# Graph layer plus experts on one core: the tiles of a three-block product pass are dealt out 11, 13, 10 instead of 10, 14, 10, and in the third block TensorE sums five tiles per product instead of four

## The reference, cut to what matters

```python
def _L1_gnn_ref(x_nodes, x_edges, path_coeffs, src, dst, path_indices):
    x1 = x_nodes[src].reshape(-1, N_SEG, EXTENT)
    x2 = x_edges.reshape(-1, N_SEG, EXTENT)
    i1, i2, i3 = (path_indices[:, 0], path_indices[:, 1], path_indices[:, 2])
    contrib = path_coeffs[None, :, None] * x1[:, i1, :] * x2[:, i2, :]
    edge_out = zeros.at[:, i3, :].add(contrib)          # 64 paths into 16 segments
    out = zeros.at[dst].add(edge_out.reshape(-1, 512))  # edges into nodes
    return out
```

## Time and profile before

| | |
|---|---|
| median of 3 runs | 276.3 us (276.22 to 276.34) |
| the profiled execution, its own time | 276.32 us |
| its span, first to last instruction | 274.5 us |
| PE busy | 263.9 us (96%) |
| DVE busy | 223.8 us (82%) |
| ACT busy | 168.5 us (61%) |
| first block, first multiply to that of the second | 89.99 to 125.48 us |
| second block | 125.48 to 181.25 us |
| third block, up to the final scatters | 181.25 to 225.77 us |
| final scatters | 225.77 to 238.95 us |

### The profile page before, as it was taken

How to read it: one execution, slowest core, us unless ns; L and a number is a source line. 1 busy time by engine, 2 the same in 40 slices (tenths; PEclk the granted TensorE clock), 3 DMA queues, 4 the chain that set the end, 5 groups by cost and what they waited for, 6 DMA issues and landing times.

```text
span 274.5 us, 5669 instructions
## 1 busy us (share of the span) xinstructions
PE 263.9 (96%) x1639; PEld 185.3 (67%) x1639; DVE 223.8 (82%) x662; ACT 168.5 (61%) x341; POOL 39.6 (14%) x52
## 2 busy tenths in 40 slices
PE   6999999999999899998999999989999989999996
PEld 4566798886444799996778786756665654468633
DVE  5977665299657999999999999999999987655272
ACT  6931341010526999978878787499999719343260
POOL 4000150060006766661000000000000000000000
PEclk9999999999999999999999999999999999999999
DMA  6699990000014755555342000014444439000002
GB/s 205 213 412 405 445 420 25 0 2 1 1 38 127 204 171 153 156 157 152 92 142 76 2 1 1 2 36 141 162 152 152 148 87 352 21 2 2 2 0 76
DMA packets 12592, 33.91 MB, mean 124 GB/s; under 512 B 3345, under 2 KB 3602, under 8 KB 12306
## 3 DMA queue, kind: packets, MB, share of 16 engines
q1 hardware_dynamic: 10482, 26.73, 27.1%
q0 software_dynamic: 2080, 6.82, 8.9%
HBM read 32.50 MB, written 1.05 MB: 122 GB/s over the span
## 4 chain that ended last, share of the span: by engine, by line
PE 83%; DVE 9%; issue 3%; ACT 2%; DVEq 1%; DMA 1%; ACTq 0%; SPq 0%
PE psum L1348 15%; PE psum L1295 14%; PE psum L1249 10%; PE psum L1351 8%; PE psum L1273 5%; DVE big L1040 4%; PE psum L1278 4%; PE psum L1301 3%; PE psum L1422 3%; PE psum L1448 3%; PE psum L1192 3%; PE psum L1178 2%; PE psum L1132 2%; PE psum L1339 2%; PE psum L1230 1%
## 5 line engine op out<-in xcount | busy, mean ns | idle before, releaser
L1295 PE MATMUL psum<-big,dst_oh 128*128 128x512 f32 x108 | 50.7, 594 | 0.5 <-DVE big L1040 0.5
L606 ACT ACTIVATE prod<-edges,coef_b 128x320 f32 (+1 forms) x78 | 43.8, 594 | 10.6 <-PE psum L1351 9.1
L1348 PE MATMUL psum<-prod,ident 128*128 128x128 f32 x160 | 32.1, 295 | 1.0 <-DVE prod L1030 0.9
L1348 PEld LDWEIGHTS psum<-prod,ident 128*128 128x128 f32 x160 | 24.5, 190 | 10.2 <-issue 9.4
L1030 DVE TENSOR_TENSOR prod<-big,prod 128x320 f32<-128x320 f32 (+1 forms) x53 | 29.4, 556 | 0.5 <-issue 0.3
L1295 PEld LDWEIGHTS psum<-big,dst_oh 128*128 128x128 f32 x108 | 18.7, 191 | 15.1 <-issue 14.3
L1249 PE MATMUL psum<-edges,big 128*128 128x256 f32 x128 | 28.3, 381 | 0.0
L1040 DVE TENSOR_TENSOR big<-big,prod 128x64 f32 (+2 forms) x80 | 26.8, 335 | 0.0
L606 ACT ACTIVATE xparts<-edges,coef_b 128x320 f32 (+1 forms) x48 | 26.1, 589 | 1.0 <-PE psum L1348 0.8
L1249 PEld LDWEIGHTS psum<-edges,big 128*128 128x128 f32 x128 | 24.1, 190 | 3.5 <-issue 0.3
L471 POOL DMA_INDIRECT big<-xn_rows,big x16 | 17.0, 1061 | 30.5 <-DMA xn_rows<-xn 23.5
(11 more groups left out here) (223 smaller groups left out, 529.4 us busy)
## 6 DMA issues: line engine op xcount, KB each, us to landing
big<-in_w SPq DMA_DIRECT2D x3, 2048.0 KB, 16.6
edges<-in_edge SPq DMA_DIRECT2D x1, 3584.0 KB, 23.9
edges<-in_f SPq DMA_DIRECT2D x7, 512.0 KB, 3.4
edges<-in_edge SPq DMA_DIRECT2D x1, 2560.0 KB, 23.7
edges<-in_edge SPq DMA_DIRECT2D x5, 512.0 KB, 3.5
edges<-in_f SPq DMA_DIRECT2D x1, 2560.0 KB, 9.8
big<-in_f SPq DMA_DIRECT2D x4, 512.0 KB, 3.6
big<-in_gnn_w SPq DMA_DIRECT2D x1, 1024.0 KB, 6.1
```

Of the source, the lines that this page charges most:

```text
L606: nc.scalar.activation(slot(n)[:, 0:BLOCKS[b], :], segment(edges_of(b), single_column(words, p)), ACT.Copy, scale=coef_b[:, p:p + 1]).then ...
L1295: last = mm(bank[2 + h], dst_oh[:, n % DR, h * P:(h + 1) * P], tile_sums(b, t), start=False, stop=False)
L1348: last = mm(path_sums(to), ident[:], product[:, 0:PT].rearrange("p t u -> p (t u)"), start=False, stop=True, skip_group_check=True)
```

## The change

The first block has 11 tiles, the second 13, the third 10. `KEPT` is [8, 6, 5]: in the third block one product of 160 columns takes five tiles, and DVE adds five tiles instead of six. The 16 segments' sums of five tiles lie three to a bank, in banks 4, 5, 6, 7, 0, 1 (`last_sums`), so PE clears six banks there and ACT makes six copies of them at the end. Because banks 0 and 1 are used again, ACT copies all six banks of the second block at one place, after the scale of path 7 (`LEAD = 8`). ACT clears five rows (`BLOCKS[2] - KEPT[2]`) instead of six. One tile of the last layer's weights `f2` moves to another room.

```diff
-    BLOCKS = [10, 14, 10]
-    FIRST = [0, 10, 24]
-    KEPT = [8, 6, 4]
+    BLOCKS = [11, 13, 10]
+    FIRST = [0, 11, 24]
+    KEPT = [8, 6, 5]
...
+    PER_BANK = 512 // (KEPT[2] * U)
...
-    LEAD, REST_LEAD = 6, 11
+    LEAD = 8
...
+        def last_sums(k):
+            b = psum[:].bitcast(mybir.dt.uint8).rearrange("p (s e) -> p s e", e=4 * U)
+            at = nc.s_assert_within((k * 171 + 2048) // 32 % 128, 0, 128 - KEPT[2], ...)
+            return b[:, bass.ds(at, KEPT[2]), :].rearrange("p o e -> p (o e)").bitcast(F32)
...
-            return [4, 5, 6, 7] + list(range(PT2[b]))
+            return [4, 5, 6, 7] + list(range(PT2[b] if b < NB - 1 else 2))
...
+                    if b == NB - 1:
+                        n = min(PER_BANK, NS - PER_BANK * i)
+                        nc.scalar.activation(
+                            kept_sums[b][:, :, PER_BANK * U * i:U * (PER_BANK * i + n)]...,
+                            bank[q][:, 0:n * KEPT[b] * U]..., ACT.Copy)\
+                            .then_inc(block_out, 1)
...
                 if b == 2 and p == LEAD - 1:
-                    copy_sums(1, 0, PT)
-                if b == 2 and p == REST_LEAD - 1:
-                    copy_sums(1, PT, 8)
+                    copy_sums(1, 0, PT + PT2[1])
...
-                    last = mm(path_sums(to), ident[:], product[:, 0:PT].rearrange("p t u -> p (t u)"),
-                              start=False, stop=True, skip_group_check=True)
-                    if KEPT[b] > PT:
+                    if b == NB - 1:
+                        last = mm(last_sums(to), ident[:], product[:, 0:KEPT[b]].rearrange("p t u -> p (t u)"),
+                                  start=False, stop=True, skip_group_check=True)
+                    else:
+                        mm(path_sums(to), ident[:], product[:, 0:PT].rearrange("p t u -> p (t u)"),
+                           start=False, stop=True, skip_group_check=True)
                         last = mm(more_sums(b, to), ident[:], product[:, PT:KEPT[b]].rearrange("p t u -> p (t u)"),
                                   start=False, stop=True, skip_group_check=True)
```

More of the change, by code:

```diff
@@ L43, in graph_and_experts @@
     PE_TILES = 8
-    PT2 = [k - PT for k in KEPT]
+    PT2 = [k - PT for k in KEPT[:2]]
+    PER_BANK = 512 // (KEPT[2] * U)
     ROW_PATHS = -(-NP // 3)
@@ L86, in more_sums @@
             return product_sums(psum[:, 0:NS * PT2[b] * U], PT2[b] * U, k)
+        def last_sums(k):
+            b = psum[:].bitcast(mybir.dt.uint8).rearrange("p (s e) -> p s e", e=4 * U)
+            at = nc.s_assert_within((k * 171 + 2048) // 32 % 128, 0, 128 - KEPT[2],
+                                    skip_runtime_bounds_check_because="three segments to a bank, six banks around the scatters")
+            return b[:, bass.ds(at, KEPT[2]), :].rearrange("p o e -> p (o e)").bitcast(F32)
         def carve(base, dt_size=4):
@@ L177, in graph_and_experts @@
         kept_sums = [sum_room[0][:, 0:KEPT[0], :], x1g[1][:, 0:KEPT[1], :], sum_room[0][:, 0:KEPT[2], :]]
-        rest_sums = [sum_room[0][:, KEPT[0]:, :], sum_room[1], sum_room[0][:, KEPT[2]:, :]]
+        rest_sums = [sum_room[0][:, KEPT[0]:, :], sum_room[1], sum_room[0][:, KEPT[2]:BLOCKS[2], :]]
         take = carve(x1g[1].rearrange("p t f -> p (t f)"))
@@ L219, in graph_and_experts @@
         ctrl_sb = take([KC, ES])
+        f2_mid = take([1, D])
         take = carve(edges[:, BLOCKS[0]:LATE, :].rearrange("p t f -> p (t f)"))
         f1_parts.append(take([KC // 2, f1.shape[1]]))
-        f2_lo = take([6, D])
+        f2_lo = take([5, D])
         f2_hi = carve(late)([FC - 6, D])
@@ L320, in f2_sb @@
         def f2_sb(c):
-            return f2_lo[:, c, :] if c < 6 else f2_hi[:, c - 6, :]
+            return f2_lo[:, c, :] if c < 5 else f2_mid[:, 0, :] if c < 6 else f2_hi[:, c - 6, :]
         x_in, idx_in, w_in, w1_in, w3_in, w2_in = (sem(n) for n in
@@ L421, in _ @@
                     .then_inc(f1_in, 16)
-            for i in range(0, 6, 2):
-                sp.wait_ge(mults, NP * (NB - 1) + 44 + 3 * i)
-                sp.dma_start(f2_lo[:, i:i + 2, :], rows(f2)[:, i:i + 2, :]).then_inc(f2_in, 16)
+            for i, (to, lo, n) in enumerate(((f2_lo[:, 0:2, :], 0, 2), (f2_lo[:, 2:5, :], 2, 3), (f2_mid, 5, 1))):
+                sp.wait_ge(mults, NP * (NB - 1) + 44 + 6 * i)
+                sp.dma_start(to, rows(f2)[:, lo:lo + n, :]).then_inc(f2_in, 16)
             sp.wait_ge(mults, NP * NB)
@@ L614, in copy_sums @@
                     act.wait_ge(psums, NP * (b + 1))
-                    if i < PT:
+                    if b == NB - 1:
+                        n = min(PER_BANK, NS - PER_BANK * i)
+                        nc.scalar.activation(
+                            kept_sums[b][:, :, PER_BANK * U * i:U * (PER_BANK * i + n)].rearrange("p t (k u) -> p k t u", u=U),
+                            bank[q][:, 0:n * KEPT[b] * U].rearrange("p (k t u) -> p k t u", t=KEPT[b], u=U), ACT.Copy)\
+                            .then_inc(block_out, 1)
+                    elif i < PT:
                         nc.scalar.activation(
@@ L1353, in _ @@
                     last.then_inc(psums, 1)
-                    if KEPT[b] > PT and b and p % 2 and p < NP - 1:
+                    if b == 1 and p % 2 and p < NP - 1:
                         mm(bank[4][:, 0:N], zero_b[:], iota_b, start=False, stop=True, skip_group_check=True)
```

## The result

The changed kernel takes **281.06 us** (median of 4 runs, 281.01 to 281.28) against 276.3 us before (4 runs too): ratio 1.0173, 95% interval 1.0161 to 1.0185, so 4.8 us slower. The prediction was 280.9 us with a range of 278.0 to 283.5 and 0.86 for slower. The profiled execution took 281.01 us, its span is 279.2 us, and the granted TensorE clock is 1.00, as before.

What follows compares the result with a forecast made beforehand. DVE bounded the kernel before; PE, late from the second block, was to set the end after the change. Final scatters at 230.4 instead of 225.77 us give +4.6, so 276.3 + 4.6 = 280.9 us, range 278.0 to 283.5.

Steps and rivals of the forecast that it cites:

- first block longer by: DVE's multiply and add each gain 32 elements in the first block, over 64 paths: +4.27 us.
- tail: From the final scatters to the end: counted at nothing; without cover by DVE's tile spacing about 1 us.
- the gather: Start of the first block: the first multiply needs a third gather, +0.35 us, bounded by 0.2 and 0.6.
- The landing rows: Earlier profile's rows for gathers, read as landing 3.4 to 3.7 us after issue; the third, issued at 86.83, lands at 90.3.
- The hand-over from ACT to DVE: Third block's start: ACT's first scale takes about 0.56 us, from 184.8, so DVE begins at 185.4.
- PE's pace in the second block: 0.474 us per path and 1.72 per scatter; PE hardly catches up, last of 11 scatters ends at 181.8, 5.1 us later.
- The border: Second to third block: clears, scales and copies follow the last scatter; PE's first product starts at 192.1, +6.4 us.
- The rival in which DVE stays the bound: All blocks: DVE sets the end, PE's third-block product starts by about 185.6; 274.5 us, chance 0.07.
- the one in which PE keeps up: Second block: PE catches up after all, only copies and wider products remain; 276.2 us, no change, chance 0.08.
- The width: Third block: a 160-column product costs 0.2755 us, on the line through 128 and 256 columns; block takes PE 38.3 us.
- The rival of a free width: Third block: wider product nearly free, PE takes 2.3 us less; 278.6 us, chance 0.05.
- the one of the register instruction: Third block: second register instruction holds PE back, 0.33 to 0.39 us per path; 284 to 288 us, chance 0.06.

Runs made afterwards that it cites:

- the third gather: Kernel before the change, its first multiply made to wait for one gather more: 277.36 us, ratio 0.9945 to the kernel before on that chip.
- the four combinations: Old or new blocks with four or five tiles per product: 276.31 and 277.26 us with 10, 14, 10; 282.04 and 281.06 us with 11, 13, 10.
- the tuned one: Changed kernel with blocks 10, 14, 10, two early scatters, copies after six scales, no fillers between third-block clears: 277.98 us, ratio 0.9963 to the kernel before.
- the disturbed runs: Three variants of the changed kernel on two other chips (swapped rooms without second-block fillers; these with earlier clears; copies after six scales): mostly 282.78 to 293.35 us.
- the first four experiments: New blocks with four-tile product, 282.04 us; old blocks with five-tile product, 277.26; changed kernel without second-block fillers, 279.80; with clears waiting for 8 scatters, 278.44.

## Why the prediction was right

The trace bears the sum out step by step:

| step | forecast | measured |
|---|---|---|
| first multiply | +0.35 | +0.78 (90.77 against 89.99) |
| first block longer by | 4.27 | 4.06 (39.55 against 35.49) |
| last scatter of the second block ends | 181.8 | 181.9 |
| first scale of the third block | 184.8 | 184.88 |
| DVE restarts | 185.4 | 185.69 |
| copies start | 188.7 | 188.80 |
| first 160-column product | 192.1 | 192.3 to 192.5 |
| five products and a scatter | 3.10 | 3.07 |
| final scatters | 230.4 | 230.66 |
| tail | 0 | -0.24 |

The time came closer (281.06 against 280.9) than its parts, and that is partly luck: the gather cost 0.43 more than forecast, and 0.21 came back in the first block and 0.24 in the tail.

**The gather** was mis-sized, beyond the upper bound of 0.6. The landing rows were added to the start of the third gather, 3.4 to 3.7 us; the first multiply started 4.0 us after it (86.77 to 90.77), and 3.98 in the kernel with nothing but that wait added. So another 0.3 to 0.4 us lie between a landing and the start of what waits for it. The hand-over from ACT to DVE was mis-sized in the same way: from the third block's first scale to DVE's first multiply it takes 0.81 us (184.88 to 185.69), not 0.56. That one cost nothing, since PE's first product hangs on ACT's copies.

**PE's pace in the second block** was the main step. From its first scatter to the end of its last it held to 0.1 us (44.5 against 44.65), and it rested on the earlier trace rows alone: 4.565 us for six paths and a scatter. Removing the fillers shows the mechanism by another edit: last scatter 1.4 us earlier, end 1.3 us earlier. What the forecast didn't split is the 0.474 us of a path; by that run 0.037 of it are fillers.

**The border** was right as a chain, last scatter, clears, scales, copies, first product. Taking the wait out of the clears gives 2.6 us back, so of the loss over half is that ACT's clears stand behind PE's last scatter, and the rest is PE's own lateness. The rival in which DVE stays the bound is refuted by the 3.58 us of idle time and by PE ending the third block 1.4 us after DVE; the one in which PE keeps up by scatters 4.56 us apart. That margin of 1.4 us is smaller than the 1.9 of the forecast, whose own terms (192.1 + 35.8 = 227.9) don't give the 228.5 written there; DVE ended at 229.23. A free width would therefore have saved about 1.4 us, not 2.3.

**The width** was right: ten rows, five products, in 1.36 us is 0.272 per product against 0.2755 from the line through 128 and 256 columns. The rival of a free width asked for 0.24, the one of the register instruction for 0.33 to 0.39. By the Trainium skill's sustained spacing ("TensorE: Matmul & The Clock Gate", "Back-to-back issue gap") 32 more columns would have added 0.017 us, an estimate from its figures; the rows show 0.050.

**The tail** was counted at nothing and gave back 0.24 us. Its first twelve rows take 5.15 us in the five undisturbed traces with the five-tile product, where PE comes to them without a wait, and 5.39 in the three in which it had waited for DVE (before, the blocks alone, the third gather).

**The parts.** I had written of one loss; the table of the four combinations shows two parts that aren't independent. The blocks alone cost 5.7 us and the product gives 1.0 of it back. The forecast held the right sum of both, but it didn't say that the product would be a loss beside the old blocks.

## What to carry to other kernels

Moving work between blocks changes not only how long each takes but which engine is late at the border; follow the slower engine's pace over the whole block, not its share of busy time, and ask what is queued behind its last instruction. Where a clear or a copy waits for the last consumer of a room, see whether it can use the part of the room that comes free first: here that is worth 2.6 us. Try the parts of a change apart and together: the five-tile product costs 1 us beside one set of blocks and saves 1 us beside the other.

## What the runs showed that I had not expected

**POOL's gathers were stretched.** In POOL's timeline of the changed kernel:

```profile
96.28 6.16 POOL L480 DMA_INDIRECT big<-xn_rows,big  x1 [0.66 <-DVE xparts L1043]
...
114.99 7.37 POOL L480 DMA_INDIRECT edges<-xn_rows,big  x1 [0.66 <-DVE xn L1043]
```

Before, none of them took more than 1.45 us. All ten traces with 11 tiles in the first block show one or more gathers of 3.1 to 16.4 us while DVE runs its multiplies and adds of 352 and 96 elements back to back; none of the four traces with 10 tiles (before, the five-tile product alone, the third gather, the tuned one) does, with DVE just as busy at 320 and 64. In all fourteen traces the second block's rows were there in time: DVE enters the block without a gap. Whether the disturbed runs lost their time by a long gather, through the gathers that then followed close together, isn't shown. The Trainium skill ("SBUF — State Buffer", "SBUF: two separate sides") says that GpSimd and VectorE share a pair of ports by an exclusive lock, taken also by a VectorE instruction with two SBUF inputs against a GpSimd operation that reads SBUF. DVE's instructions here have two SBUF inputs and a gather takes its indices from there, so the rule may be at work. No run here shows it, and it doesn't say why 352 and 96 elements should shut POOL out for microseconds and 320 and 64 not.

**ACT stood still for no engine.** In the disturbed runs and, for 3.1 us, in the tuned kernel at 95 to 98 us, ACT's idle time is put down to nothing on this core. In the traces of the first chip (before, the change, the first four experiments) there is no such stretch; on the two other chips seven of eight traces have one, all but the third gather's. DMA rows in these stretches name instruction queues beside the gathers: this is the view of DMA queues (packets, MB, share of 16 engines) of the tuned kernel between 92 and 101 us:

```profile
q0 software_dynamic: 433, 1.38, 55.4%
q8 instruction: 1, 0.02, 1.0%
```

A fetch of instructions that comes late behind crowding gathers would explain it. The Trainium skill ("Runtime: NRT & Kernel Launch", "Instruction fetch mechanics") has each sequencer fetch its next block of instructions over a DMA queue of its own, a cost it calls mostly hidden. Here this is argued only. The same queue rows stand in undisturbed traces too, the changed kernel had an even higher DMA share between 131 and 140 us (0.82 against 0.58) without a stall, and no run took the fetch or the gathers away.

**A filler costs little more than half of what it seems to.** 0.11 us of filling product behind every second path would be 0.055 per path; by the pace it is 0.037, since a 128-column product right behind a 64-column one takes 0.05 us more than behind the filler. Over the whole stretch, 1.8 us for 27 fillers, it is 0.066 each.
